# Whole value products at the end of four-tile head slots that hold a chunk

## What is computed

```python
xn = _group_norm(x, scale, bias)
qkv = jnp.einsum('bhwc,cd->bhwd', xn, w_qkv)
q, k, v = ...                                   # per head, 1024 positions
scores = jax.nn.softmax(jnp.einsum('bcq,bck->bqk', q, k) * hd ** -0.5, axis=-1)
o = jnp.einsum('bqk,bck->bqc', scores, v)
out = jnp.einsum('bhwc,cd->bhwd', o, w_out) + b_out
return out + skip
```

## Time and profile before

| what | us |
|---|---|
| median of 3 runs | 2286.01 (2283.77 to 2286.83) |
| the profiled execution | 2283.49 |
| its span, first to last instruction | 2281.7 |
| outside the span | 1.8 |

### The profile page before, as it was taken

How to read it: one execution, slowest core, us unless ns; L and a number is a source line. 1 busy time by engine, 2 the same in 40 slices (tenths; PEclk the granted TensorE clock), 3 DMA queues, 4 the chain that set the end, 5 groups by cost and what they waited for, 6 DMA issues and landing times.

```text
span 2281.7 us, 41605 instructions
## 1 busy us (share of the span) xinstructions
PE 2145.4 (94%) x16748; PEld 1152.1 (50%) x16748; DVE 1687.5 (74%) x3104; ACT 1445.8 (63%) x1698; POOL 408.4 (18%) x541
## 2 busy tenths in 40 slices
PE   5999999999999999999999999999999998999999
PEld 3444343444633367333763347533475334745888
DVE  6899898889688866787668876788767866772433
ACT  1577676776477754777458774577646875477554
POOL 3102201220121311112120221203111030021131
PEclk7899999999999999999999999999999999999999
DMA  5404133140312213040230402204040050000000
GB/s 136 87 9 92 41 67 73 32 93 3 68 37 60 35 29 74 11 82 13 52 61 2 94 2 60 54 2 94 2 87 17 2 88 7 6 6 1 5 6 19
DMA packets 48590, 97.45 MB, mean 43 GB/s; under 512 B 7824, under 2 KB 10640, under 8 KB 48272
## 3 DMA queue, kind: packets, MB, share of 16 engines
q1 hardware_dynamic: 48400, 94.81, 20.0%
HBM read 55.98 MB, written 37.75 MB: 41 GB/s over the span
## 4 chain that ended last, share of the span: by engine, by line
PE 73%; DVE 19%; issue 4%; ACT 2%; POOL 1%; DMA 1%; SPq 0%; POOLq 0%; ACTq 0%; DVEq 0%
PE outs L1339 17%; PE work L1285 16%; DVE part_max L1077 14%; PE outs L1379 10%; PE pairs L1357 8%; PE pairs L1313 6%; PE pairs L1201 5%; PE work L1210 5%; PE pairs L1210 3%; PE work L1207 1%; DVE o_turn L1089 1%; DVE stats L1015 1%; ACT probs L966 1%; DVE neg_max L1109 1%; DVE oT L1104 1%
## 5 line engine op out<-in xcount | busy, mean ns | idle before, releaser
L1077 DVE TENSOR_REDUCE part_max<-work 128x1 f32<-128x512 f32 x2048 | 1283.2, 681 | 228.2 <-PE work L1285 223.1
L966 ACT ACTIVATE probs<-pairs 128x1024 f32<-128x1024 f32 x1024 | 1004.8, 1022 | 375.3 <-PE pairs L1313 362.9
L1285 PE MATMUL work<-k_stack,q_stack 62*128 62x512 f32 x2048 | 726.4, 461 | 31.9 <-DVE part_max L1077 26.1
L1313 PE MATMUL pairs<-q_stack,k_stack 64*128 64x512 f32 x2048 | 604.0, 438 | 11.1 <-DMA q_stack<-shift_parts 9.4
L1285 PEld LDWEIGHTS work<-k_stack,q_stack 62*128 62x128 f32 x2048 | 316.5, 187 | 552.8 <-DVE part_max L1077 407.9
L1339 PE MATMUL outs<-probs,v_heads 128*32 128x256 f32 (+1 forms) x5448 | 588.6, 497 | 6.8 <-DVE o_turn L1089 6.7
L1109 DVE TENSOR_REDUCE neg_max<-pairs 128x1 f32<-128x1024 f32 x128 | 156.6, 1224 | 254.7 <-PE pairs L1357 254.6
L1313 PEld LDWEIGHTS pairs<-q_stack,k_stack 64*128 64x128 f32 x2048 | 273.6, 186 | 61.1 <-ACT probs L966 38.6
L973 ACT ACTIVATE probs<-pairs,neg_max 128x1024 f32<-128x1024 f32 x128 | 142.6, 1114 | 244.8 <-DVE neg_max L1109 244.8
L1379 PE MATMUL outs<-v_full,probs 128*128 128x128 f32 x2048 | 258.4, 279 | 4.8 <-issue 4.8
L1379 PEld LDWEIGHTS outs<-v_full,probs 128*128 128x128 f32 x2048 | 241.3, 192 | 37.4 <-issue 34.2
(11 more groups left out here) (126 smaller groups left out, 1121.2 us busy)
## 6 DMA issues: line engine op xcount, KB each, us to landing
k_scratch<-parts SPq DMA_DIRECT2D x64, 256.0 KB
q_scratch<-parts SPq DMA_DIRECT2D x64, 256.0 KB
k_stack<-k_scratch SPq DMA_DIRECT2D x64, 256.0 KB, 6.9
q_stack<-q_scratch SPq DMA_DIRECT2D x64, 256.0 KB, 9.8
k_stack<-k_scratch SPq DMA_DIRECT2D x64, 128.0 KB, 8.5
q_stack<-q_scratch SPq DMA_DIRECT2D x64, 128.0 KB, 10.7
q_stack<-shift_parts SPq DMA_DIRECT2D x256, 4.0 KB
tmp<-x SPq DMA_DIRECT2D x7, 512.0 KB, 3.5
```

The costliest lines, as they stand in the source:

```text
L966: nc.scalar.activation(probs[:, plan.prob[u], 2 * n:2 * n + 2, :], pairs[:, plan.half["pair", t], :, :], ACT.Exp, scale=HEAD_SCALE).then_i ...
L1077: nc.vector.tensor_reduce(part_max[:, r % 2, column:column + 1], bank_of(("tile", r, n)), AX_X, ALU.max, negate=True).then_inc(tile_max, 1)
L1285: nc.tensor.matmul(bank_of(("tile", r, n)), qs[rows, i, a, heads, P * t:P * (t + 1)], ks[rows, i, keys, heads, :], start=True, stop=True). ...
L1313: last = nc.tensor.matmul(pairs[:, plan.half["pair", t], half, :], ks[rows, i, key // QT, first + n, P * (key % QT):P * (key % QT + 1)], q ...
```

## The change

The pattern for four or more tiles with a chunk loses its U. The values of these slots are then one whole item at the V step (`("values", n - 1, 0, 2)`).

```diff
-    CHUNK_PATTERNS = {0: "PPCV", 1: "TPPCV", 2: "TPTPCV", 3: "TPTPTCV", 4: "TPTCUTPTV"}
+    CHUNK_PATTERNS = {0: "PPCV", 1: "TPPCV", 2: "TPTPCV", 3: "TPTPTCV", 4: "TPTCTPTV"}
```

## The result

| what | before | after |
|---|---|---|
| median, runs of one comparison | 2285.49 us (2283.77 to 2286.83, 4 runs) | 2300.49 us (2296.11 to 2305.55, 4 runs) |
| ratio, 95% interval | | 1.0069 [1.0050, 1.0087] |
| the profiled execution | 2283.49 | 2305.55 |
| its span | 2281.7 | 2303.8 |
| mean granted clock of TensorE in it | 0.986 | 0.978 |

The change makes the kernel 15.0 us slower, 0.69%. The forecast was slower by 10.9, with a range of 2287.5 to 2303.0: side and range held, but 4 us of the 15 were not in the sum.

What follows compares the result with a forecast made beforehand. PE, busy 94% of the span with 73% of the chain, was named as the bound; waits the change exposes were priced slot by slot: 7.6 + 5.2 - 0.6 - 0.1 - 1.2 = +10.9, 2286.0 + 10.9 = 2296.9 us, range 2287.5 to 2303.

Steps and rivals of the forecast that it cites:

- (a): 37 slots with one k, q or v chunk and pairs: P2 waits for exp(P1), together +7.6 us.
- I take 0.96: PE's stream: the undivided chunk followed by a tile lasts 0.96 us, within bounds of 0.86 to 1.06.
- Counting four changes in either order: PE's stream: both orders have four tiling-mode changes a slot, so by that rule the sum is near zero.
- The stream alone would thus gain about 0.04 to 0.05: PE's own items in the 81 slots: 0.04 to 0.05 us gained a slot, under 4 us in all.
- (b): 12 slots with gn1 or gn2 alone: U covered the fourth tile's wait for DVE; +0.43 each, +5.2 us.
- (c): Four slots without pairs: +0.28 each, -0.42 in the slot behind; net -0.6 us in four.
- (d): Nine slots with a transposing chunk: P2's wait is shorter; between -0.14 and +0.08 each, sum -0.1 us.
- (e): 19 other slots (out chunks, two chunks, five tiles): P2 follows exp(P1) in either order; stream gain -0.8 us.
- -0.4 for DVE's smaller backlog: Slots behind the 19 others: DVE enters less far behind, giving back 0.4 us.
- absorbed: Rival: later slots wait less for DVE, so two thirds or more return; 2286 to 2290 us, chance 0.13.
- Sum: 7.6 + 5.2 - 0.6 - 0.1 - 1.2: Whole kernel: the terms of all classes of the 81 slots added up, +10.9 us.
- PE's idle time for weight loads ahead of pairs, ended by ACT, rises by about 0.3 in some 30 places.: Sign in the profile: PE's idle time ahead of pairs, ended by ACT, grows about 0.3 in some 30 places.

Runs made afterwards that it cites:

- e7: The changed kernel with the exponential of P1 done on half of its elements in the 37 k, q or v slots; 2293.77 us, 1.0039 of before.
- e4: The changed kernel with the chunks of four-tile slots again in four products of 32 columns, values still whole; 2299.96 us, 1.0062 of before.
- e9: The kernel before, with both halves of the values behind the last tile in the 12 norm slots only; 2296.76 us, 1.0050 of before.
- second comparison: The changed kernel unaltered, run once more beside before; 2301.52 us to 2287.09, ratio 1.0060.
- e11: Whole values in the 12 norm slots only, plus a throw-away filler product of 256 columns ahead of each norm product; 2293.16 us, 1.0024 of before.
- e5: The kernel before, halves kept, with the chunks of slots with four or more tiles undivided; 2306.09 us, 1.0096 of before.
- e3: The kernel before with whole values only in the 32 slots that are neither plain k, q, v nor norm slots; 2282.98 us, 0.9992 of before.
- e1: The kernel before with whole values only in the 37 four-tile slots with one k, q or v chunk and pairs; 2291.71 us, 1.0031 of before.
- e8: The kernel before with whole values in 69 of the 81 slots, the 12 norm slots keeping halves; 2288.05 us, 1.0006 of before.
- e10: The kernel before with the split order also given to 42 four-tile slots without a chunk that had whole values; 2292.13 us, 1.0025 of before.
- e2: The kernel before with whole values only in the 12 four-tile slots with one gn1 or gn2 chunk; 2294.03 us, 1.0047 of before.

## Why the prediction was right, and where it was wrong

**P2's wait (a): right.** P2 at 1.90 to 1.91 against a forecast of 1.91 (all but the first of these slots), the slot 3.55 to 3.58 against 3.57 where no shift or late tile is in it, +7.5 against +7.6; `e7` takes the cause away and 5.0 of the 7.5 go.

**The undivided chunk: mis-sized.** "I take 0.96" was the term. It lasts 1.05 to 1.06 up to a tile, the upper bound, and 1.09 for a `v` chunk, above it. The row that it was taken from, was the wrong neighbour: what follows the chunk there is 128 x 128 like the chunk, so no change of placement lies behind it, and `e4` prices such a change at 0.11 (0.89 to 1.00). Counting four changes in either order gives zero, and that is right for a chunk by columns: 1.00 and values of 1.00 in `e4`, against 0.89 + 0.54 + 0.57 before. The undivided form takes 0.06 on top. The sum didn't suffer, since exp(P1) sets P2, but the lone tile is 0.18 and not "about 0.3" ahead of P2, and the wait's share of (a) is two thirds, not all. "The stream alone would thus gain about 0.04 to 0.05" is refuted by sign: in `e7`, where only the stream is left, the slot is 3.39, 0.06 longer than before.

**The norm slots (b): right in the slot.** +0.43 each, the fourth tile where it was. `e9` shows that it is their place behind DVE's maximum.

**The slots without pairs (c), transposing slots (d) and (e): right** within 0.1 us each.

**"-0.4 for DVE's smaller backlog": mis-sized.** It is about -3.8 us. About a dozen slots behind `out` and `up` slots went from 2.30 to 2.13. The rival "absorbed" was true as a mechanism, and gave back 30% of the 12.7 us of (a) and (b), not two thirds.

**The clock: not in the sum.** "Sum: 7.6 + 5.2 - 0.6 - 0.1 - 1.2" has no such term. It is worth 16.6 us more at half clock x 0.325 = 5.4 of the 15.0, in the second comparison 18.9 x 0.325 = 6.1 of 14.4, either known to about 2.6. Of the three parts of the change, the norm slots alone bring it. The remaining +9.7 +- 1.7 at equal clock agrees with the forecast of +10.9; by the measured slots it should be 7.5 + 5.2 - 0.6 - 0.8 - 3.8 = 7.5, and the 2 us between are not shown. So a forecast of 10.9 was near to 15.0 because the missing clock and a give-back that was too small, errors of about 5 and 3.4, pull against each other. That part of the hit is luck; the two waits that carry the sum are not.

**A sign that didn't show.** "PE's idle time for weight loads ahead of pairs, ended by ACT, rises by about 0.3 in some 30 places." The weight loads ahead of pairs, before and then after:

```profile
L1313 PEld LDWEIGHTS pairs<-q_stack,k_stack 64*128 64x128 f32 x2048 | 273.6, 186 | 61.1 <-ACT probs L966 38.6 <-DMA q_stack<-shift_parts 11.7 <-issue 1.8
```

```profile
L1313 PEld LDWEIGHTS pairs<-q_stack,k_stack 64*128 64x128 f32 x2048 | 270.6, 187 | 58.2 <-ACT probs L966 34.5 <-DMA q_stack<-shift_parts 11.2 <-issue 1.8
```

It fell from 38.6 to 34.5 us, though the wait is real. The weight loads after, in the slot shown above:

```profile
429.55 0.18 PEld L1285 LDWEIGHTS work<-k_stack,q_stack 62*128 62x128 f32 x1 [0.76 <-DVE part_max L1077]
429.74 0.19 PEld L1313 LDWEIGHTS pairs<-q_stack,k_stack 64*128 64x128 f32 x2
```

The third tile's load lasts 0.18, as long as P2's wait, and stands right ahead of P2's load, so no idle time is left between them. The wait is seen in the distances between starts, nowhere in the sums. Where the 4 us less come from is not shown.

**What stays open:** through what the norm slots lower the clock (the filler points at PE's wait, no more), why `e5` has as much time at half clock without them, and the 2 to 3 us at equal clock that the whole change has above its slots and its parts. No kernel here beats the one before beyond its noise: `e3`, the nearest, is 0.9992 [0.9977, 1.0006].

## What to carry to other kernels

Before an item is moved off a place where it "only" fills PE's stream, list what is waiting for another engine right behind it, and by which ring: the half of the values here gained nothing of itself, and what it covered was worth 0.14 us in each of 37 slots (P2's wait, by `e7`) and 0.43 in each of 12. Price a slot by the distances between starts, and then look one slot further, since an engine that is less far behind gives time back there, and one that is further behind takes it. And compare the granted clock of every run before the slots: here about a third of the loss was clock, and came with 12 of the 81 slots, those in which the fourth tile waits for VectorE behind a tiny product.

## What the runs showed of the hardware that was not expected

- The clock: kernels whose norm slots are changed spend 87 to 97 us at 1.2 GHz (78 with the filler). Four kernels whose norm slots keep their order (before, `e1`, `e3`, `e8`) spend 71 to 73. But `e5`, which changes only the placement of the chunk, has 96.8, by the means 25.5 +- 5.4 above before beside it, so norm slots are not the only way to it (`e10` with 77.9 is within the noise of before). A us at half clock costs this kernel 0.325 us. The Trainium skill, "TensorE: Matmul & The Clock Gate", section "A second HAM failure mode: psum-queue depth-cycling", tells of a kernel whose clock oscillates because TensorE idles for moments between groups of products while it cycles through banks; `e2` and `e11` agree in direction, but the busy shares above (0.85 ahead of the fall, 0.83 where none came) don't tell the two apart.
- Two halves of the values, 256 columns each, cost 1.00 us next to each other, as a whole does, and 0.54 + 0.57 with a tile and a pair between them.
- A chunk of 512 columns costs 0.89 us by columns ahead of values, 1.00 by columns ahead of a tile, and 1.05 to 1.06 undivided ahead of either (`k` and `q`; `v` 1.09).
- ACT's end reaches PE as a start 0.05 us later, in the changed kernel at all but one P2 of (a).
